# Softmax normalization moved from a pass after attention to each chunk boundary inside it, in a four-layer kernel on eight cores

## What is computed

```
x = x + attn_a(ln(x))   # causal softmax attention, 16 heads of 64
x = x + ffn(ln(x))      # full softmax attention, 16 heads of 64,
                        # projections with a low-rank mixture part
x = x + attn_b(ln(x))   # gated retention scan, no softmax
x = x + ffn(ln(x))      # as above, same weights

# both softmax layers, per head:
scores = q @ k.T * scale          # causal mask in attn_a only
attn   = softmax(scores, axis=-1)
out    = attn @ v                 # then heads joined, out projection
```

## Time and profile before

| | |
|---|---|
| Median of 11 runs | 4251.44 us |
| Lowest and highest | 4231.56 and 4497.31 us |
| Profiled execution: time | 4243.35 us |
| Profiled execution: span of the slowest core (7) | 4241.8 us |
| Spans of the eight cores | 4205.8 to 4241.8 us |
| Mean granted TensorE clock of core 7 | 0.818 of full |
| Causal attention, head pair 0 to the last exponential | about 267 to 979 us |
| ffn attention, first and second | about 1413 to 2251 and 3270 to 4108 us |

### The profile page before, as it was taken

The page is one execution under the profiler, slowest core; times in us unless marked ns, Lnnn a source line. Parts: engine busy times, 40 slices in busy tenths (PEclk is TensorE's granted clock), DMA queues, the critical chain, the costliest instruction groups (busy, mean ns, idle before and its releaser), DMA issues. The chain is left out here.

```text
span 4241.8 us, 40783 instructions; the slowest of 8 cores (4205.8 to 4241.8 us)
## 1 busy us (share of the span) xinstructions
PE 3135.1 (74%) x13815; PEld 1290.0 (30%) x13815; DVE 1439.3 (34%) x2007; ACT 1484.1 (35%) x1488; POOL 65.2 (2%) x81
## 2 busy tenths in 40 slices
PE   3678877788537788888888646546366888888888
PEld 1223333334213233333325212122132333333334
DVE  5323333335462211111115554542742111111124
ACT  0024444451000466666671000030001666666650
POOL 0000000000000000000000000000000000000000
PEclk7668887879758898888888868778578888888889
DMA  2110010002512000000002611016122000000014
GB/s 91 20 15 6 6 11 6 1 1 80 178 30 30 6 6 6 6 5 6 1 1 56 202 20 20 0 20 195 62 40 25 6 6 6 6 6 1 1 40 139
DMA packets 91213, 144.39 MB, mean 34 GB/s; under 512 B 62057, under 2 KB 70394, under 8 KB 78604
## 3 DMA queue, kind: packets, MB, share of 16 engines
q1 hardware_dynamic: 18108, 104.04, 7.4%
q0 software_dynamic: 72912, 37.75, 6.7%
HBM read 145.97 MB, written 33.55 MB: 42 GB/s over the span
## 5 line engine op out<-in xcount | busy, mean ns | idle before, releaser
L735 ACT ACTIVATE ringf<-psd,negcb 128x1024 bf16<-128x1024 f32 x1024 | 1059.5, 1124 | 602.4 <-PE psd L683 602.0
L735 ACT ACTIVATE ringa<-psd,negcb 128x1024 bf16<-128x1024 f32 x320 | 337.4, 1116 | 366.7 <-PE psd L683 337.9
L663 PE MATMUL psb<-ringf,vprf 128*65 128x512 bf16 x1024 | 445.9, 435 | 10.5 <-ACT ringf L735 9.2
L680 PE MATMUL psd<-qpairf,kpairf 64*128 64x512 bf16 x1024 | 422.6, 425 | 29.0 <-ACT ringf L735 6.4
L683 PE MATMUL psd<-qpairf,kpairf 64*128 64x512 bf16 x1024 | 430.3, 432 | 0.0
L667 PE MATMUL psb<-ringf,vprf 128*65 128x512 bf16 x1024 | 423.2, 413 | 0.0
L637 PE MATMUL psb<-c_IDENT,densf 1*128 1x1 f32 x1024 | 170.1, 291 | 172.4 <-DVE act L837 172.4
L680 PEld LDWEIGHTS psd<-qpairf,kpairf 64*128 64x128 bf16 x1024 | 91.8, 95 | 459.7 <-issue 458.5
L637 PEld LDWEIGHTS psb<-c_IDENT,densf 1*128 1x128 f32 x1024 | 166.5, 250 | 189.8 <-issue 189.8
L183 ACT ACT_TABLE_LOAD x4 | 5.1, 1283 | 575.5 <-DVE lnrcf L178 321.0
L663 PEld LDWEIGHTS psb<-ringf,vprf 128*65 128x65 bf16 x1024 | 114.1, 111 | 302.0 <-issue 294.3
(11 more groups left out here) (250 smaller groups left out, 4187.4 us busy)
## 6 DMA issues: line engine op xcount, KB each, us to landing
lnstf<-Xs SPq DMA_DIRECT2D x16, 1024.0 KB, 5.5
xof<-Xs SPq DMA_DIRECT2D x16, 1024.0 KB, 6.7
lnsta<-xT SPq DMA_DIRECT2D x8, 1024.0 KB, 6.1
xoa<-xT SPq DMA_DIRECT2D x8, 1024.0 KB, 6.7
Xs<-xna SPq DMA_DIRECT2D x8, 1024.0 KB, 8.7
Xs<-xnf SPq DMA_DIRECT2D x8, 1024.0 KB, 8.8
lnstb<-Xs SPq DMA_DIRECT2D x8, 1024.0 KB, 4.9
xob<-Xs SPq DMA_DIRECT2D x8, 1024.0 KB, 7.6
```

What stands on the lines that cost most here:

```text
L663: t.matmul(PSB[4][0:65, :], VP[tkpv][:, hA * 65:hA * 65 + 65], RING[slot][:, 0:512], start=(tkpv == 0), stop=(tkpv == n - 1))
L680: t.matmul(pd[:, 0:512], KP[p % 2][0:64, ks], QP[p % 2][0:64, cs], start=True, stop=True, tile_position=(0, 0))
L735: ex.inc(s.activation(RING[slot][:], pd[:], AF.Exp, bias=NEGC[:, p:p + 1], scale=softmax_scale))
```

## The change

The columns, their reciprocals and the whole pass of 64 broadcasts and multiplications after attention go. In their place, at each chunk boundary:

- ScalarE, after the first exponential of the next chunk, waits for `v_ce` and computes the reciprocals of the two denominator rows in place as exp(-ln(d)): an Ln over 1x1024 fp32 elements, then an Exp with scale -1 (`den_recip`). The Exp increments a new counter `s_nd`.
- TensorE broadcasts each 1x512 row over 64 partitions of PSB[6] with an fp32 matmul against a row of ones (`emit_rank1`). The first is placed after the scores of key tile 1 and waits for `s_nd`; the second after the scores of tile 3 and the PV product of tile 1, and waits until VectorE has used the first.
- VectorE multiplies the 64x512 part of `act2` by PSB[6] in place, after key tiles 2 and 3 (`norm_mult`).
- After the last chunk of a layer all of this runs once more, with nothing of the next chunk beside it.
- The projection's matmuls no longer wait for a normalization.

```diff
-            def emit_colify(p, c):
-                t.wait_ge(vce.sem, B["vce"] + p * NC + c + 1)
...
-                        last = t.matmul(
-                            DEN[:, col:col + 1],
-                            DENS[0:1, half * 2 * CH + h01 * CH + sub * 128:
-                                 half * 2 * CH + h01 * CH + (sub + 1) * 128],
-                            bufs["IDENT"][0:1, 0:1], start=True, stop=True)
-                td.inc(last)
+            def emit_rank1(cc, h01):
+                half = cc % 2
+                if h01 == 0:
+                    t.wait_ge(snd.sem, B["snd"] + cc + 1)
+                else:
+                    t.wait_ge(vnm.sem, B["vnm"] + 2 * cc + 1)
+                tnb.inc(t.matmul(
+                    PSB[6][0:64, :], bufs["ONESROW"][0:1, 0:64],
+                    DENS[0:1, half * 2 * CH + h01 * CH:
+                         half * 2 * CH + (h01 + 1) * CH],
+                    start=True, stop=True))
...
-                        if tk == 0 and col_pend:
-                            emit_colify(*col_pend.pop(0))
+                        if tk == 1 and norm_pend:
+                            emit_rank1(norm_pend[0], 0)
+                        if tk == 3 and norm_pend:
+                            emit_rank1(norm_pend.pop(0), 1)
...
+            def den_recip(cc, step):
+                half = cc % 2
+                dh = DENS[0:1, half * 2 * CH:half * 2 * CH + 2 * CH]
+                if step == 0:
+                    s.wait_ge(vce.sem, B["vce"] + cc + 1)
+                    P.smark(s.activation(dh, dh, AF.Ln))
+                else:
+                    P.sjoin(s)
+                    snd.inc(s.activation(dh, dh, AF.Exp, scale=-1.0))
...
+                        if tk == 0 and sden_pend:
+                            den_recip(sden_pend[0], 0)
+                            den_recip(sden_pend.pop(0), 1)
...
+                def norm_mult(h01):
+                    ccn = vnorm_pend[0]
...
+                    v.wait_ge(tnb.sem, B["tnb"] + 2 * ccn + 1 + h01)
...
+                    vnm.inc(v.tensor_tensor(sl, sl, PSB[6][0:64, :], ALU.mult))
...
+                        if tk == 2 and vnorm_pend:
+                            norm_mult(0)
+                        if tk == 3 and vnorm_pend:
+                            norm_mult(1)
...
-                        v.wait_ge(td.sem, B["td"] + cc - 1)
+                        v.wait_ge(tnb.sem, B["tnb"] + 2 * (cc - 2) + 2)
...
-        if do_cn:
-            @blk.vector
-            def _(v):
-                P.vmark(v.reciprocal(bufs["RECIP"][:], PSB[6][:, 0:256]))
...
-                                last = t.matmul(
-                                    PSB[bank][0:64, sub * 128:(sub + 1) * 128],
-                                    rp[:, col:col + 1].broadcast_to([128, 64]),
-                                    bufs["IDENTB"][:],
...
-                        vn.inc(v.tensor_tensor(sl, sl, PSB[bank][0:64, :],
-                                               ALU.mult))
...
             def _(t):
-                t.wait_ge(vn.sem, vn0 + ncn)
```

More of the change, by code:

```diff
@@ L537, in emit_attention @@
     ts, ex, vm, pv = P.c("t_s"), P.c("s_ex"), P.c("v_m"), P.c("t_pv")
-    vce, td = P.c("v_ce"), P.c("t_d")
+    vce, snd = P.c("v_ce"), P.c("s_nd")
+    tnb, vnm = P.c("t_nb2"), P.c("v_nm2")
     B = dict(tqk=tqk.v, vev=vev.v, snc=snc.v, ts=ts.v, ex=ex.v,
-             vm=vm.v, pv=pv.v, vce=vce.v, td=td.v)
+             vm=vm.v, pv=pv.v, vce=vce.v, snd=snd.v, tnb=tnb.v, vnm=vnm.v)
     aq0 = [aq[0].v, aq[1].v]
@@ L628, in _ @@
         def _(t):
-            def emit_colify(p, c):
-                t.wait_ge(vce.sem, B["vce"] + p * NC + c + 1)
[L631 to L636, removed]
-                        last = t.matmul(
-                            DEN[:, col:col + 1],
-                            DENS[0:1, half * 2 * CH + h01 * CH + sub * 128:
-                                 half * 2 * CH + h01 * CH + (sub + 1) * 128],
-                            bufs["IDENT"][0:1, 0:1], start=True, stop=True)
-                td.inc(last)
+            def emit_rank1(cc, h01):
[9 more added lines that the diff above has]
+                    start=True, stop=True))
             for g in range(11):
                 t_qk_group(t, 0, g)
-            col_pend = []
+            norm_pend = []
             TS_MAP = {0: 0, 1: 1, 2: 2, 3: 3, 4: 4, 5: 5, 6: 6, 7: 7,
@@ L701, in _ @@
                             t_qk_group(t, p + 1, qkq.pop(0))
-                    col_pend.append((p, c))
-            while col_pend:
-                emit_colify(*col_pend.pop(0))
+                    norm_pend.append(p * NC + c)
+            while norm_pend:
+                cc = norm_pend.pop(0)
+                emit_rank1(cc, 0)
+                emit_rank1(cc, 1)
         @blk.scalar
@@ L742, in _ @@
                             si[0] += 1
+                    sden_pend.append(p * NC + c)
                 if not done_negc[0]:
                     negc_math(p + 1)
+            while sden_pend:
+                cc = sden_pend.pop(0)
+                den_recip(cc, 0)
+                den_recip(cc, 1)
         ev_state = {}
@@ L800, in _ @@
                       8: 8, 9: 9, 10: 10, 11: 11, 14: 12}
+            vnorm_pend = []
             for p in range(NP):
@@ L803, in _ @@
                 vi = [0]
+                def norm_mult(h01):
+                    ccn = vnorm_pend[0]
+                    pn, cn_ = ccn // NC, ccn % NC
+                    h = 2 * pn + h01
+                    v.wait_ge(tnb.sem, B["tnb"] + 2 * ccn + 1 + h01)
+                    sl = ACT2[h // 2][(h % 2) * 64:(h % 2) * 64 + 64,
+                                      cn_ * CH:(cn_ + 1) * CH]
+                    vnm.inc(v.tensor_tensor(sl, sl, PSB[6][0:64, :], ALU.mult))
+                    if h01 == 1:
+                        vnorm_pend.pop(0)
                 for c in range(NC):
@@ L839, in _ @@
                                       c * CH:(c + 1) * CH], PSB[5][0:64, :]))
+                    vnorm_pend.append(cc)
                     if c == NC - 1:
@@ L842, in _ @@
                             v_evgroup(v, p + 1, evq.pop(0))
+            while vnorm_pend:
+                norm_mult(0)
+                norm_mult(1)
 def emit_ctxnorm(P, bufs, tag):
```

37 lines of the change are left out of this document (1 added, 36 removed).

## The result

The change makes the kernel slower: 4520.76 us median of 12 runs (4488.09 to 4649.01) against 4254.93 for the kernel before beside it. The ratio is 1.062, 95% interval 1.0592 to 1.0646. In some executions the cores of one die, or of both, are granted a lower clock, so all ratios here compare only executions without that, while the medians in us are over all. I forecast 4320 us and a range up to 4400: the sign is right, the size is 3.7 times too small (+266 us against +72). The time is that of my fourth rival, 4455, and somewhat beyond it. The profiled execution took 4523.05 us; all rows of after are from its slowest core, 6.

What follows compares the result with a forecast made beforehand. No engine was full over the span; TensorE's order was taken as the bound at chunk boundaries. 177 us lost there plus 12 in tails, less 117 saved at projections, gave +72 us, said as 4320 us; range 4222 to 4400.

Steps and rivals of the forecast that it cites:

- Rival 4: Chunk boundaries: second broadcast keeps clock low until +17 us; 3.6 and 3.0 us lost per boundary, 4455 us; chance 0.15.
- The projection: Start of the output projections: weights late next, 19.4 us after their issue; 117 us saved in all.
- Ln and Exp: ScalarE's reciprocals at chunk boundaries: 1.09 and 1.05 us, ending at +5.2 us from S0's start, no table load.
- The first broadcast: Between S1 and S2 at a boundary, behind the wait for ScalarE: 1.85 us, bounded by 0.9 and 2.0.
- S2: Third scores of a chunk, counting from S0: start at +7.15 us from S0's start, 1.1 us late.
- The second broadcast: After S3 and PV1 at a boundary: begins near +10.1 us from S0's start, 1.77 us at low clock.
- VectorE's multiplications: At chunk boundaries: priced at 0.68 us each, filling idle VectorE, so the second broadcast's wait costs nothing.
- The causal boundaries: 24 chunk boundaries of the causal attention stage: 1.7 us lost at each, 41 us in sum.
- The tail of the causal stage: From a stage's last evictions to the next block: 3.9 us lost, three times, 12 us.
- The step that failed: Clock return at a boundary: 5.1 us after the new S2, at +12.2 us from S0's start.
- my 2.0 us: 62 chunk boundaries: S5 2.0 us late at each, second broadcast wholly or mostly at low clock; 124 us lost.
- The other terms: Outside the boundaries: 117 us saved at the projections, 12 us lost in the stage tails.

Runs made afterwards that it cites:

- e4: The kernel before with the normalization pass ahead of the three output projections left out, output unnormalized: ratio to before 0.9755.
- e2: The changed kernel with the second broadcast and its multiply moved from key tile 3 to 9 in the f layers: ratio to before 1.0165, 4303.3 us.
- e3: The changed kernel with the same fp32 broadcasts over 128 rows, 127 of them zeros, instead of one row: ratio to before 1.0203.
- e10: The changed kernel with both fp32 broadcasts side by side at key tile 1, ahead of S2, and one joint multiply: ratio to before 1.0024.
- e11: The changed kernel with both broadcasts in bf16, side by side at key tile 1, ahead of S2, and one joint multiply: ratio to before 0.9755, 4142.05 us.
- e6: The changed kernel with bf16 reciprocals and bf16 broadcasts in the same two places: ratio to before 1.0044, 4256.56 us median.
- e1: The changed kernel without ScalarE's Ln and Exp, the broadcast waiting for VectorE's evictions instead: ratio to before 0.987.
- e5: The changed kernel without both broadcasts and both multiplications, ScalarE's Ln and Exp kept, output unnormalized: ratio to before 0.9371, 3974.44 us.
- e7: The changed kernel, fp32, with reciprocals after the fourth exponential and broadcasts behind tiles 5 and 7 in chunks of more than four tiles: ratio to before 0.9573.
- e12: The kernel before with its columns moved behind key tile 5 in chunks of more than 4 tiles: 4070.25 us in one comparable execution.
- e8: The changed kernel with late, side-by-side bf16 broadcasts and one joint multiply, Ln and Exp behind the fourth exponential: ratio to before 0.9189.

## Why the prediction was right and wrong

**Right.** The projection: 104 us (e4) against 117, weights as the new releaser, 19.7 us after their issue against 19.4. Ln and Exp: 1.05 us each against 1.09 and 1.05, ending at +5.22 against +5.2, with no table load. The first broadcast, 1.93 us against 1.85, and S2 at +7.24 against +7.15. The second broadcast starts at +10.3 against +10.1 and takes 1.96 us against 1.77. VectorE's multiplications, 0.68 us, end before anything inside the f stages waits for them: the 1.9 us that TensorE waits for VectorE there are 0.93 in each of the two tails. The causal boundaries: 2.1 us each (cores 0 to 3) against 1.7. The tail of the causal stage: from the end of the last eviction to the next block 8.4 us where the end of the first f stage took 4.0, +4.4 against 3.9.

**The step that failed** is the one after them: "The clock comes back ... 5.1 us after the first scores that follow the columns ...; counted from the new S2, at +12.2." That term was mis-sized: I took 5.1 us from a boundary in which nothing but scores and PV products followed the columns, and used it for one with 1.96 us of one-row matmul inside. One boundary stood for all there, too, but that did little: over the 31 of before the low stretch is 2.8 to 6.8 us, mean 5.5. The clock came back at +16.7, 9.5 us after S2 and 4.5 after S4, the first scores behind the second broadcast. Rival 4 had both the mechanism and the place (+17); I gave it 0.15, although I had already let decide that one-row matmuls don't raise the clock. If they don't raise it, a rise can't be counted on across one either. What separates the two readings is shown by e2 (moved away: 5.0), e3 (128 rows in its place: 5.5), e10 and e11 (ahead of S2: 5.5 and 5.6) and e6 (only 0.6 us long, still 8.7). e2 and e3, in which this step is mended in the f stages, come out at ratios of 1.017 and 1.020, and my 4320 over the median of 4251 is 1.016. That they meet it so closely is partly luck: in both the second broadcast ran mostly at full clock, which my 2.0 us didn't assume, and the causal term was too small.

**What it was worth.** Per boundary 4.8 us instead of 2.0 in the f stages, and 2.1 instead of 1.7 in the causal one: on cores 0 to 3 363 us instead of 177. The other terms, -117 + 12 = -105, came out at -94 there. The median span of these cores grew by 271 us, 199 more than my 72; 186 of the 199 are boundaries, 175 of them in the f stages. (Between the slowest cores the sums are 384 - 104 = 280, with the 27 us in the causal stage that most cores don't have.) Rival 4 forecast 316 us at the boundaries, and its total is near for two errors that partly cancel. Its 3.0 us in the causal stage was too high. Its 3.6 us in the f stages was too low: it counted three more slow steps of 0.5 us; the low stretch was 4.9 us longer on average and up to 13.3 us long, and groups of the next head pair's projections can fall into it (eight matmuls take 3.59 us instead of 1.89).

**Clock and activity.** In the f stage of after TensorE was busy 802 us at a mean clock of 0.78, in that of before 731 us at 0.87. The Trainium skill (TensorE: Matmul & The Clock Gate, "What's actually happening") says that activity releases the throttle. For the one-row matmuls the traces again don't agree, with a low stretch of 10.4 us in after; for e3's 128-row ones they do, with 5.5.

**Parts that I didn't price.** I costed the longer wait at its length alone. In e1, with 2.3 us less of it, the first broadcast often ran at full clock, and the low stretch fell to 6.7 us with 7 boundaries at 1.3 us or less. And I costed ScalarE's Ln and Exp only through the first broadcast, not through the exponential behind them (e5). How the 319 us of e1 divide into wait and clock isn't settled: the mean low stretch counts both.

## What to carry to other kernels

Don't put a matmul of one or a few rows into the stretch in which TensorE recovers from a stall: beside its own length it costs the later return of the clock, which was the larger part of the 3.1 us per boundary that e2 won back; put it directly ahead of the work that follows the stall (e10, e11) or well behind it (e2, e7). What waits for another engine belongs in TensorE's queue behind work that can already run: moving the same instructions by four tiles, and ScalarE's part by three exponentials, was worth 10% here (e7 against after), and moving the columns some 4% in the kernel before (e12). The same holds for ScalarE's queue (e5 against e8). And when the time a clock takes to return is read from one sequence, ask whether the new sequence still holds the same work.

## What was not expected of the hardware

- The clock came back over 128-row fp32 matmuls of which 127 rows were zeros (e3: mean low stretch 5.5 us, 9.2 to 9.5 at 6 boundaries) and not over one-row matmuls in the same places (after: 10.4 us, 13.1 to 13.3 there).
- Two one-row matmuls into different partition halves, with tile positions side by side, run together: four fp32 instructions took 1.97 us (e10), two alone 1.93 us (after), both at half clock; the bf16 pair took 0.40 to 0.43 us (e8, e11).
- After the same idle 2.5 us, the clock had fallen at one boundary and not at the next (e1).
